# A four-layer hybrid image model on one core: row statistics moved into the stages that write the rows, and three steps of the DPP attention moved between engines

## The reference, cut to what matters

```python
sim = k @ q_i                                   # 128 tokens of the sequence here: 256
sim = where(arange(Tn) <= i, sim, -inf)
_, top_idx = top_k(sim, 8)                      # the eight best earlier tokens: slots
slot_is_i = (top_idx == i) & slot_valid
# all 8 single slots and all 28 pairs of slots, each together with token i itself:
valid = slot_valid[slots].all(axis=1) & ~slot_is_i[slots].any(axis=1)
score = log(where(valid, det(gram of the 2 or 3 keys), 1) + 1e-6) / (s + 1)
out_s = softmax(K @ q_i / 4) @ V
probs = softmax(where(valid, score, -1e30))
y = out_s of the best one        # v[i] where none is valid
```

## Time and profile before

| | |
|---|---|
| time, median of 3 runs | 6769.15 us (6767.99 to 6771.01) |
| the profiled execution's own time | 6724.65 us |
| its span in the profile | 6722.8 us |
| TensorE / VectorE / ScalarE / GpSimd busy | 72% / 69% / 40% / 21% |
| mean granted TensorE clock | 0.757 of full speed |

### The profile page before, as it was taken

One profiled execution on the slowest core, in us unless ns is written; L12 is line 12 of the kernel. 1 busy time (PEld: TensorE's weight loads), 2 busy tenths in 40 slices (PEclk: granted clock), 3 DMA queues, 4 the chain that ended last, 5 costly groups with the idle time before them and its releaser, 6 DMA issues. The chain is left out here.

```text
span 6722.8 us, 139374 instructions
## 1 busy us (share of the span) xinstructions
PE 4869.4 (72%) x46024; PEld 3804.2 (57%) x46025; DVE 4616.6 (69%) x10128; ACT 2706.9 (40%) x9057; POOL 1390.5 (21%) x1125
## 2 busy tenths in 40 slices
PE   5777777967777777777777777765089498419995
PEld 2333334755666566656665666555068376419995
DVE  4777774238999999999999999994267734312224
ACT  3343342224554545454555455543322133233331
POOL 1323322110000000000000000000655200166663
PEclk7777778986767676777676767665589799559997
DMA  8000000002111111121111111121122600221114
GB/s 144 7 5 8 5 3 6 0 8 76 71 71 65 69 68 71 65 71 65 71 69 68 66 70 71 65 71 27 65 71 76 113 0 6 73 67 45 46 46 137
DMA packets 226734, 370.27 MB, mean 55 GB/s; under 512 B 104818, under 2 KB 187355, under 8 KB 201028
## 3 DMA queue, kind: packets, MB, share of 16 engines
q1 hardware_dynamic: 200036, 309.26, 15.6%
q0 software_dynamic: 26112, 53.64, 2.4%
HBM read 287.04 MB, written 75.78 MB: 54 GB/s over the span
## 5 line engine op out<-in xcount | busy, mean ns | idle before, releaser
L2680 PE MATMUL l2a_g<-l2a_feat,l2a_onehot 128*128 128x33 bf16 x27648 | 783.1, 184 | 414.0 <-ACT l2a_values L2283 211.2
L2680 PEld LDWEIGHTS l2a_g<-l2a_feat,l2a_onehot 128*128 128x128 bf16 x27648 | 768.1, 101 | 484.6 <-issue 238.3
L2546 DVE TENSOR_REDUCE l2a_dots<-l2a_prod 128x144 f32<-128x2304 f32 x192 | 489.6, 2550 | 4.5
L1912 PE MATMUL l_y<-l_hc,l_selT 128*96 128x512 f32 x384 | 296.3, 866 | 264.2 <-POOL l_hc L1750 263.6
L2629 PE MATMUL l2a_s<-l2a_qkT 32*128 32x128 f32 (+1 forms) x1536 | 484.5, 451 | 0.0
L2652 PE MATMUL l2a_m<-main_ident,l2a_pv 128*96 128x128 f32 x2304 | 339.4, 319 | 148.6 <-DVEq L2487 148.6
L2652 PEld LDWEIGHTS l2a_m<-main_ident,l2a_pv 128*96 128x96 f32 x2304 | 331.4, 201 | 169.4 <-issue 166.1
L1750 POOL TENSOR_TENSOR l_hc<-l_hs,l_bc 128x512 f32<-128x512 f32 x192 | 243.6, 1269 | 718.8 <-DVE l_hs L1817 718.8
L2554 DVE TENSOR_SCALAR l2a_onehot<-l2a_spread,l2a_pos 128x4096 bf16<-128x4096 bf16 x288 | 360.8, 1281 | 43.7 <-DVE l2a_hd L2448 20.1
L2629 PEld LDWEIGHTS l2a_s<-l2a_qkT 32*128 32x128 f32 x1536 | 309.2, 249 | 86.0 <-issue 38.3
L713 PE MATMUL l3f_expert_h<-l3f_tT,l3f_w_own 96*128 96x256 f32 x2592 | 334.2, 288 | 8.6 <-POOL l3f_w_own L670 6.7
(11 more groups left out here) (408 smaller groups left out, 11353.8 us busy)
## 6 DMA issues: line engine op xcount, KB each, us to landing
l2a_spread<-l2a_idx_rows SPq DMA_DIRECT2D x192, 1024.0 KB, 4.7
rows_in<-main_zeros SPq DMA_DIRECT2D x1, 13824.0 KB, 82.7
l2f_xg<-rows_in SPq DMA_DIRECT2D x72, 192.0 KB, 2.5
l3f_xg<-rows_in SPq DMA_DIRECT2D x72, 192.0 KB, 2.5
l2f_combine_y<-rows_out SPq DMA_DIRECT2D x32, 384.0 KB, 3.8
l3f_combine_y<-rows_out SPq DMA_DIRECT2D x32, 384.0 KB, 4.8
l3f_w<-in_l3f_w SPq DMA_DIRECT2D x2, 4608.0 KB, 32.2
l_xT<-in_l_xT SPq DMA_DIRECT2D x16, 384.0 KB, 3.8
```

The lines of the kernel that those rows point to most:

```text
L1912: nc.tensor.matmul(y_ps[:, :], selT[:, g, :], hc[:, g % 2, :], start=g == 0, stop=g == G - 1).then_inc(hc_used, 1)
L2546: nc.vector.tensor_reduce(dots[:, quad_of(s[2]), 0:NPROD], prod[:, :, :, :], AX.X, ALU.add).then_inc(S["dots_ready"], 1)
L2680: ins = nc.tensor.matmul(o[:, a * FEAT:a * FEAT + 2 * HS + 1], onehot[:, kt, at:at + P], feat3[:, s[1], kt, part, h, 0:2 * HS + 1], start= ...
```

## The change

Three things are altered. (1) `late` of `l1` and of `l3a` makes, right after it has written an image's two tiles, mean and variance of them with the new `moments_of_image` (two `bn_stats`, two `bn_aggr`, one copy on VectorE); the passes over all tiles at the head of `l2a` and of `l3f`'s routing fall away. (2) In the DPP attention `find` writes only `mark` (1000 where a slot is gone, in bf16); ScalarE casts the places to bf16 (`place`), and TensorE adds both while it turns them; `gone` is made from `mark` by ScalarE in `extend`. The two additions that make `veto` for pairs go from VectorE's `det_stage` to GpSimd. (3) `add_out` stands at the end of a VectorE body.

```diff
-def moment_steps(nc, dve, stats, stats_ready, moments_ready, x_res, moments):
+def moment_steps(nc, dve, stats, stats_ready, moments_ready, x_res, moments, known):
+    if known:
+        dve.sem_inc(moments_ready, TILES)
+        return
     for t in range(TILES):
         nc.vector.bn_stats(stats[:, t, :], x_res[:, t, :]).then_inc(stats_ready, 1)
     for t in range(TILES):
         dve.wait_ge(stats_ready, t + 1)
         nc.vector.bn_aggr(moments[:, t, :], stats[:, t, :]).then_inc(moments_ready, 1)
+
+def moments_of_image(nc, dve, held, stats, tile_stats, tile_moments, x_res, moments, n):
+    for t in range(2):
+        nc.vector.bn_stats(stats[:, t, 0:6], tile_of(x_res, n, t)).then_inc(tile_stats, 1)
+    for t in range(2):
+        dve.wait_ge(tile_stats, n * 2 + t + 1)
+        hold(dve, held)
+        nc.vector.bn_aggr(stats[:, t, 6:8], stats[:, t, 0:6]).then_inc(tile_moments, 1)
+    dve.wait_ge(tile_moments, n * 2 + 2)
+    hold(dve, held)
+    nc.vector.tensor_copy(moments[:, bass.ds(n * 2, 2), :], stats[:, :, 6:8])
```

ScalarE in the DPP attention:

```diff
                 def extend(n, u, t):
-                    nc.scalar.copy(gone[:, t, :, SLOTS:], gone[:, t, :, 0:EXT - SLOTS])
+                    for at in (slice(0, SLOTS), slice(SLOTS, EXT)):
+                        nc.scalar.activation(gone[:, t, :, at].rearrange("p (j i) a -> p j i a", j=QUAD),
+                                             mark[:, t, :, :, 0:at.stop - at.start].rearrange("p i j a -> p j i a"),
+                                             ACT.Copy, scale=-1e27)
                     nc.scalar.copy(top[:, t, :, SLOTS:], top[:, t, :, 0:EXT - SLOTS]).then_inc(S["extended"], 1)
...
                         q = count_of((n, u, i))
+                        act.wait_ge(S["scored"], counted(q * 2 + 2))
+                        act.wait_ge(S["idx_found"], counted(q * 2 + 2))
+                        act.wait_ge(S["idxT_psum"], counted(q))
+                        nc.scalar.copy(place[:, :, :], idx[:, :, :]).then_inc(S["placed"], 1)
                         act.wait_ge(S["idxT_psum"], counted(q + 1))
```

GpSimd:

```diff
+                def vetoes(n, u, t):
+                    r = n * 2 + t
+                    pool.wait_ge(S["extended"], counted(r + 1))
+                    pool.wait_ge(S["most_ready"], counted(r))
+                    hold(pool, S["pool_held"])
+                    out = gone[:, t, :, :]
+                    nc.gpsimd.tensor_tensor(veto[:, :, 1:4, :], lo(out, 3), wrapped(out, 1, 3), ALU.add)
+                    nc.gpsimd.tensor_tensor(veto[:, :, 4, 0:4], out[:, :, 0:4], out[:, :, 4:8], ALU.add
+                                            ).then_inc(S["veto_ready"], 1)
...
-                    if s and ((nxt and i == 4) or (i < 2 and in_range(n))):
+                    if s and ((nxt and i == 4) or (i < 2 and in_range(n)) or stage(back, 2)):
                         pool.wait_ge(S["prod_ready"], count_of(s) + 1)
                         hold(pool, S["pool_held"])
+                    if stage(back, 2):
+                        vetoes(*stage(back, 2))
                     if nxt and i == 4:
                         squares(*nxt)
```

VectorE, in `det_stage`, `log_stage`, `find` and `body`:

```diff
-                    send(TT(veto[:, :, 1:4, :], lo(out, 3), wrapped(out, 1, 3), ALU.add))
-                    link(TT(veto[:, :, 4, 0:4], out[:, :, 0:4], out[:, :, 4:8], ALU.add))
...
                     dve.wait_ge(S["log_ready"], counted(r + 1))
+                    dve.wait_ge(S["veto_ready"], counted(r + 1))
...
+                    dve.wait_ge(S["placed"], counted(q))
                     for j in range(QUAD):
...
-                    nc.vector.tensor_scalar(out, idx[:, :, :], pos[:, t:t + 1], -1e30, ALU.is_ge,
-                                            ALU.mult).then_inc(S["mask_chain"], 1)
-                    dve.wait_ge(S["mask_chain"], q + 1)
-                    nc.vector.scalar_tensor_tensor(out=idxm[:, :].rearrange("p (j a) -> p j a", j=QUAD), in0=out,
-                                                   scalar=-1e-27, in1=idx[:, :, :], op0=ALU.mult,
-                                                   op1=ALU.add).then_inc(S["idxm_ready"], 1)
+                    nc.vector.tensor_scalar(mark[:, t, i % QUADS, :, :], idx[:, :, :], pos[:, t:t + 1], 1000.0,
+                                            ALU.is_ge, ALU.mult).then_inc(S["marked"], 1)
...
-                    if stage(back, OUT):
-                        add_out(*stage(back, OUT))
                     nxt = next_image(n, u, last)
...
                     if back(2):
                         sums(back(2))
+                    if stage(back, OUT):
+                        add_out(*stage(back, OUT))
```

TensorE:

```diff
-                    pe.wait_ge(S["idxm_ready"], counted(q + 1))
+                    pe.wait_ge(S["placed"], counted(q + 1))
+                    pe.wait_ge(S["marked"], counted(q + 1))
                     pe.wait_ge(S["idxT_ready"], counted(q))
...
-                    nc.tensor.matmul(m_ps[0:QUAD * SLOTS, 0:P], idxm[:, :], ident_bf[:, :], start=True,
+                    nc.tensor.matmul(m_ps[0:QUAD * SLOTS, 0:P], mark[:, i // QUADS, i % QUADS, :, :], ident_bf[:, :],
+                                     start=True, stop=False)
+                    nc.tensor.matmul(m_ps[0:QUAD * SLOTS, 0:P], place[:, :, :], ident_bf[:, :], start=False,
                                      stop=True).then_inc(S["idxT_psum"], 1)
```

More of the change, by code:

```diff
@@ L312, in _ @@
                 dve.wait_ge(tables_in, 64)
-                moment_steps(nc, dve, stats, stats_ready, moments_ready, x_res, moments)
+                moment_steps(nc, dve, stats, stats_ready, moments_ready, x_res, moments,
+                             from_probabilities and consts["known"]["l3f"])
                 rstd_steps_dve(nc, dve, chain, half_log, moments, y0, norm["rstd"],
@@ L1167, in _ @@
                 nc.vector.memset(keys[HC:HC + 1, :, 1, :], 1.0).then_inc(ones_ready, 1)
-                moment_steps(nc, dve, stats, stats_ready, moments_ready, x_res, moments)
+                moment_steps(nc, dve, stats, stats_ready, moments_ready, x_res, moments, False)
                 dve.wait_ge(folded, 1)
@@ L1212, in late @@
                     chain.close()
+                    hold(dve, dve_held)
+                    moments_of_image(nc, dve, dve_held, tile_parts, tile_stats, tile_moments, x_res, moments, n)
                 pipelined_late(dve, first, rest, late)
@@ L1345, in fourier_phase @@
         y_used = m.sem("y_used")
+        tile_stats = m.sem("tile_stats")
+        tile_moments = m.sem("tile_moments")
+        dve_held = m.sem("dve_held")
+        stats = m.sb("stats", [P, 2, 8])
         with nc.Block() as block:
@@ L1401, in late @@
                                             ALU.add).then_inc(y_used, 1)
+                    dve.wait_ge(y_used, counted(n + 1))
+                    hold(dve, dve_held)
+                    moments_of_image(nc, dve, dve_held, stats, tile_stats, tile_moments, x_res, moments, n)
                 def rest(n, u, nxt, before):
@@ L2019, in dpp_attention_phase @@
         idx = m.sb("idx", [P, QUAD, SLOTS], U32)
-        idxm = m.sb("idxm", [P, QUAD * SLOTS], BF16)
+        place = m.sb("place", [P, QUAD, SLOTS], BF16)
+        mark = m.sb("mark", [P, 2, QUADS, QUAD, SLOTS], BF16)
         idxT = m.sb("idxT", [QUAD * SLOTS, P], BF16)
@@ L2359, in _ @@
             def _(dve):
-                for name in ("own_ready scored idx_found idxm_ready onehot_ready dots_ready bent_ready diff_ready "
+                for name in ("own_ready scored idx_found marked onehot_ready dots_ready bent_ready diff_ready "
                              "det_ready denom_ready most_ready pv_ready x_added").split():
                     dve.sem_inc(S[name], 1)
-                moment_steps(nc, dve, stats, S["stats_ready"], S["moments_ready"], x_res, moments)
+                moment_steps(nc, dve, stats, S["stats_ready"], S["moments_ready"], x_res, moments,
+                             consts["known"]["l2a"])
                 chain0 = Chain(dve, S["dve_chain0"])
@@ L2403, in det_stage @@
                     self_sim = own[:, u, t, :]
-                    sim, out = top[:, t, :, :], gone[:, t, :, :]
+                    sim = top[:, t, :, :]
                     dve.wait_ge(S["dots_ready"], counted(n * STEPS + (t + 1) * QUADS))
@@ L2416, in det_stage @@
                     send(TT(most[:, :, :], sim, over(self_sim, EXT), ALU.max))
-                    send(TT(both[:, :, :, :], lo(away[:, :, :]), hi(away[:, :, :]), ALU.mult))
-                    send(TT(veto[:, :, 1:4, :], lo(out, 3), wrapped(out, 1, 3), ALU.add))
-                    link(TT(veto[:, :, 4, 0:4], out[:, :, 0:4], out[:, :, 4:8], ALU.add))
+                    link(TT(both[:, :, :, :], lo(away[:, :, :]), hi(away[:, :, :]), ALU.mult))
                     send(nc.vector.tensor_copy(mx[:, :, 0, :], most[:, :, 0:SLOTS]))
@@ L2833, in build @@
                   "rows_in": rows_in, "rows_out": rows_out, "zeroed": zeroed,
```

(1 more changed line is left out.)

15 lines of the change are left out of this document (9 added, 6 removed).

## The result

The changed kernel takes 6696.47 us, median of 4 runs (6691.49 to 6705.19), the kernel before 6768.71 in the same comparison: a ratio of 0.9894, 95% interval 0.9877 to 0.9911, 72 us less. The forecast was 6712 in a range of 6662 to 6752.

A forecast was written before the change was run, and what follows sets the result against it. VectorE, busy 94% of the DPP loop, was taken as the bound. The terms -76 (marks and vetoes), +37 given back, -21 and +3 (statistics) sum to -57, from the median 6769.15 to 6712 us, range 6662 to 6752.

The forecast's parts named there:

- marks: In the DPP loop's `find`, one instruction in place of L2518 and L2521: 0.23 us 192 times, -45 us (-27 to -52).
- vetoes: In the DPP det stage, two additions leave VectorE's queue for GpSimd: 0.48 us 64 times, -31 us.
- `add_out`: In the DPP body, the same instruction later in VectorE's queue: 0 us (-13 to +13).
- given back: lengthened instructions: In the DPP loop, TensorE about 1.1 us later, so GpSimd's `squares` and `split_low` block VectorE: +37 us (0 to +60).
- given back: waits for the logs: In the DPP loop, no cost; VectorE waiting for ScalarE's logs was named as a sign of a time above 6712.
- `l3f` head, `l2a` head: Statistics gone: -21 us at the head of `l3f`, 0 at `l2a`, where VectorE's cast waits for the `pos` load.
- the tails: Behind the last images of `l1` and `l3a`, nothing covers the moved statistics: +3 us (2 to 5).
- The 3 for `split_low`: In the DPP loop, GpSimd's `split_low` slides against VectorE as `squares` does: +3 us of the +37.
- A: DPP loop: TensorE's lateness is made up in the turn's waiting time, `squares` stays: -94, 6675 us; chance 0.25.
- B: DPP loop: everything VectorE gains is lost to GpSimd's blocking: -18, 6751 us; chance 0.13.
- C: DPP step 2: TensorE becomes the bound at a clock of 0.75, step 17.3 us: +27, 6796 us; chance 0.05.
- D: Head of `l2a`: its statistics pay as well if the front end begins before the loads: 21 more, 6691 us; chance 0.05.

The follow-up runs named there:

- the early cast: The changed kernel with ScalarE's cast to `place` behind the copies of the second head of four instead of the fourth: 6660.88 us, ratio 0.9844.
- the control: The kernel before, with no edit, run and profiled once more: 6770.07 us, ratio 1.0004.

## Why the prediction was right, point by point

The sign, the range and the mechanism held; three terms of the sum were off: the marks were worth 18 us more, what was given back by blocking was 9 less, and waits for the logs, priced at nothing, took 16. That the third took back more than half of the first two is luck, and the total came out 15 us below the forecast. Terms of VectorE's queue are measured from the start of an instruction to the start of the next, over the whole loop.

| term | forecast | measured |
|---|---|---|
| marks: last search, L2518 and L2521 against search and `mark`, without lengthening | -45 | -63 |
| vetoes | -31 | -31 |
| `add_out` | 0 | 0 alone, 45 as cover |
| given back: lengthened instructions | +37 | +28: 31 in the weigh stage, 3 less than before at `mark` |
| given back: waits for the logs | 0 | +16 |
| other gaps of VectorE's queue | 0 | -4 |
| DPP loop | -39 | -54 |
| `l3f` head, `l2a` head | -21, 0, and +3 for the tails | -19.3, +2.5 |

**Marks.** This term is mis-sized. The forecast took one row, where L2521's follower started 0.11 us behind it. Over 192 steps the follower came 0.21 us behind it (40.6/192) and L2521 0.28 behind L2518 (67.2 less 12.7 of lengthening, over 192), 0.50 together; `mark` leaves 0.24 (55.7 less 9.9, over 192), not 0.15. The last search of a step also hands over 0.07 us sooner (13.7/192). That is 0.33 a step and not 0.23. Putting the instruction back cost 66.6 us.

**Vetoes.** Right to the microsecond, and they do lie beside the sum at no cost. What the forecast did not see is that a shorter det stage makes VectorE wait for ScalarE's logs, so that their net worth was 16 (the run with the vetoes back).

**What is given back.** Right in place and cause, a quarter too much in size. Of the 37, 34 were for `squares`: 1.5 us an image, 46 in all, less 13 that L2518 lost already. The runs show 31 in the weigh stage less 10 at `mark`, so 21; the 31 fell to 2 and to 6 when the turn no longer waited for the cast (two runs), and to nothing when `squares` lay elsewhere. The 3 for `split_low` were 7 (1.7 to 8.9). This went only with `idxm` back on VectorE (0.9); it stayed with the early cast, with `squares` moved and with the vetoes back (8.6, 8.3, 8.3), so the lateness of the turn is not its cause, and what is was not tried. One reading was wrong: L2518 and `squares` had not blocked each other before, since GpSimd's instructions kept their times there (L2324 826 to 829 ns); only VectorE was held.

The forecast also put the logs at nothing. With the turn late, ScalarE waits longer for the front end (for TensorE's product ahead of `qkT` 177 us before, 238 after, 185 with the early cast), and the logs are among its next jobs; the early cast took 16 us of log waits away, so the lateness is their cause, and the way by the front end is read from the code's order and these waits. The forecast named that wait as a sign that the time would lie above 6712. It came, and the time lay below, since the marks were worth 18 more and blocking cost 9 less.

**`add_out`.** The number was right and the reason incomplete. The forecast followed the late turn to the scores and the front end, and not to the projection that stands between them on TensorE. Had the change left `add_out` where it was, the forecast of 6712 would have been 24 us too low (6735.89), and the term 45.

**Statistics.** `l2a` 0 and `l3f` -21 held; the tails were 2.5 and about 1.7 (20.98 less 19.3). In `l3a` the times per trace, 299 to 306 in four traces without the statistics and 302 to 308 in ten with them, show no cost clear of their spread. In `l1` the traces differ by more than the 1 us in question.

**Rivals.** A (no collisions) is refuted by the rows of L2516. B needed 76 us given back; 44 were (28 and 16). C's condition nearly came about and its consequence did not: the granted clock of step 2, median over the images, was 0.76 after and 0.89 before, but 0.78 in the control as well, and step 2 took 14.5 us after against 15.3 in both. So the price that C put on that clock, 17.3 us for the step, did not come; VectorE stayed at 94%, and its waits for scores did not grow (3.3 us against 3.4). D is refuted by the cast's wait and by the statistics alone.

## What to carry to other kernels

Follow a wait that is moved to everything behind it on its engine, and price each consumer's margin: here a turn that starts 0.8 us later on an engine with a quarter of its time free cost some 20 us of blocking two engines away and 16 us of waits for logs, and would have cost some 32 more at an add that had 0.43 us of margin. When two preparations lie beside each other, removing one can show next to nothing until the other goes too. The price of an instruction in a queue is the mean interval to its follower over all its uses, not one row.

## What the runs showed of the hardware that was not expected

GpSimd's `squares` and VectorE's two-operand products lengthen each other (826 to 1345 ns, 552 to 1212 ns), while the same `squares` beside a one-input reduction of 2.55 us lengthens neither. A `tensor_scalar` of 128 x 32 with a uint32 input, 241 ns alone, took up to 1456 ns beside `split_low`, to 0.04 us behind its end, and did not lengthen it. Loads with two weights of 97 partitions ran at 25 GB/s for most of 24 us, and with these split into 96 partitions and one at up to 415. The two routing stretches were 15 us or more longer in every later trace than in the first trace of before, with 128 scattered writes of the same length in each; the cause stays open.
